# Final sum on 128 partitions with x1 and L stored channel by channel; v tiles asked for first while mixing

## What is computed

```python
x = x + L0(gn(x))      # gn: group norm, 16 groups of 3 channels, no affine
x = x + L1(gn(x))

# L0: qkv = 3x3 depthwise(1x1(x)); q, k, v in 8 heads of 6 channels, each 4x4 pixel
#     block unfolded to 96 rows per head x 16384 columns; q, k normalised along columns
attn = softmax(einsum('bhcn,bhdn->bhcd', q, k) * temperature)   # 96 x 96 per head
out  = einsum('bhcd,bhdn->bhcn', attn, v)                       # then fold back, 1x1 projection

# L1: four scans of 512 steps, each step a 5-tap convolution over the other axis
nxt = inp + conv1d(carry, w, b)    # down, then up (rows); right, then left (columns)
```

## Time and profile before

| | |
|---|---|
| median of 3 runs | 11776.97 us (11760.05 to 11849.2) |
| the profiled execution | 11759.42 us, span 11757.6 us |
| PE, DVE, ACT, POOL busy | 81%, 72%, 58%, 24% of the span |
| DMA, mean over the span | 187 GB/s (2199.76 MB) |
| mean granted TensorE clock | 0.913 |

### The profile page before, as it was taken

The page is one execution under the profiler, slowest core; times in us unless marked ns, Lnnn a source line. Parts: engine busy times, 40 slices in busy tenths (PEclk is TensorE's granted clock), DMA queues, the critical chain, the costliest instruction groups (busy, mean ns, idle before and its releaser), DMA issues. The chain is left out here.

```text
span 11757.6 us, 213657 instructions
## 1 busy us (share of the span) xinstructions
PE 9564.5 (81%) x72742; PEld 9137.6 (78%) x72742; DVE 8439.2 (72%) x15908; ACT 6855.6 (58%) x11561; POOL 2842.7 (24%) x4104
## 2 busy tenths in 40 slices
PE   0899999999999978878689989998999899980000
PEld 0899999999999966656489989998899899980000
DVE  8677777777777756656677777776899877765445
ACT  0677777677777733323266658998333366654444
POOL 0000000000000000000056656665566566650000
PEclk9999999999999988888899999999999999995555
DMA  8666666666666659988766657776666567769999
GB/s 346 120 131 132 132 129 132 120 132 130 133 130 131 132 124 207 213 189 204 176 200 208 217 184 194 209 212 175 200 207 218 181 196 211 212 196 290 281 272 278
DMA packets 697798, 2199.76 MB, mean 187 GB/s; under 512 B 57233, under 2 KB 549489, under 8 KB 602657
## 3 DMA queue, kind: packets, MB, share of 16 engines
q1 hardware_dynamic: 597344, 2097.84, 69.3%
q10 hardware_dynamic: 100352, 100.67, 3.4%
HBM read 1409.77 MB, written 788.53 MB: 187 GB/s over the span
## 5 line engine op out<-in xcount | busy, mean ns | idle before, releaser
L1193 POOL TENSOR_TENSOR down_lo<-down_o_t,down_hi 112x256 fp32r<-112x256 f32 x1024 | 706.4, 690 | 5978.7 <-ACT down_hi L1238 5586.9
L472 PE MATMUL conv_ps<-tap_high,x_high 128*128 128x432 f32 (+2 forms) x6144 | 1884.6, 307 | 43.9 <-DVE x_edge L548 30.1
L472 PE MATMUL conv_ps<-tap_low,x_high 128*128 128x432 f32 (+2 forms) x6144 | 1908.1, 311 | 0.0
L472 PE MATMUL conv_ps<-tap_high,x_low 128*128 128x432 f32 (+2 forms) x6144 | 1906.4, 310 | 0.0
L352 ACT ACTIVATE x_high<-raw,negmean 128x512 fp32r<-128x512 f32 x1024 | 1214.6, 1243 | 61.2 <-DMA raw_edge<-x 49.4
L544 DVE SCALAR_TENSOR_TENSOR x_low<-raw,negmean,x_high 128x512 fp32r<-128x512 f32 x1024 | 1148.6, 1150 | 120.8 <-ACT x_high L352 120.8
L472 PEld LDWEIGHTS conv_ps<-tap_high,x_high 128*128 128x128 f32 x6144 | 1161.6, 189 | 66.1 <-DVE x_edge L548 31.7
L472 PEld LDWEIGHTS conv_ps<-tap_high,x_low 128*128 128x128 f32 x6144 | 1166.4, 190 | 22.5
L472 PEld LDWEIGHTS conv_ps<-tap_low,x_high 128*128 128x128 f32 x6144 | 1162.8, 189 | 20.7 <-issue 0.2
L1363 DVE TENSOR_TENSOR fin_out<-fin_rows,fin_l 48x2048 f32<-48x2048 f32 x256 | 585.2, 2286 | 623.0 <-DMA out<-fin_out 352.5
L883 DVE TENSOR_TENSOR scan_t_b<-o_ps,res_b 48x1024 f32<-48x1024 f32 x512 | 625.7, 1222 | 560.7 <-PE o_ps L796 557.1
(11 more groups left out here) (191 smaller groups left out, 26410.6 us busy)
## 6 DMA issues: line engine op xcount, KB each, us to landing
raw<-x SPq DMA_DIRECT2D x764, 256.0 KB, 5.5
x_scan<-scan_t_b SPq DMA_DIRECT2D x64, 1792.0 KB, 16.5
down_u_in<-x_scan SPq DMA_DIRECT2D x64, 1792.0 KB, 15.4
d_rows<-down_o_t SPq DMA_DIRECT2D x32, 3584.0 KB, 24.3
u_cols<-up_o_t SPq DMA_DIRECT2D x64, 1792.0 KB, 14.5
right_u_in<-u_cols SPq DMA_DIRECT2D x32, 3584.0 KB, 16.6
r_cols<-right_o_t SPq DMA_DIRECT2D x32, 3584.0 KB, 24.4
left_u_in<-r_cols SPq DMA_DIRECT2D x32, 3584.0 KB, 16.7
```

Source lines behind the costliest of these rows:

```text
L472: nc.tensor.matmul(bank(dy, side, lo - side, hi - side), xs[at], ws[taps], start=fresh[side], stop=False, skip_group_check=True)
L1193: nc.gpsimd.tensor_tensor(lo[:, b, 1:LP + 1], state(k // T, k, b), hi[:, b, k % 2, 1:LP + 1], ALU.subtract).then_inc(lo_ready[b], 1)
```

## The change

- `x1_scan` becomes (B, C, G, 2, T, W2) and `l_rows` (B, C, G, 2, W/T, 8, T): channel by channel, without dead rows. A channel's data is 1 MiB from the next one's. So the store of x1 (mixing) and the load of it (down) are DMAs of 48 partitions for each half, and left's store runs 512 bytes at a time.
- `final_sum` cuts x1, L and the result into 24 equal chunks of 4 MiB, each 128 partitions x 32 KB, adds them with four adds of 128x2048 per chunk, straight from x1's and L's order; ScalarE's copies are gone. Stores are issued from ScalarE's queue.
- Mixing: SyncE asks for v one group further ahead and before it waits for sums; the residual is loaded as two blocks of 8 whole rows, so a channel's part is one run of 16 KB; the sums become four adds of 48x512.
- The down scan clears the dead rows of `u_in` on GpSimd and loads its first groups before the taps.
- Tiles needed only before the scans are released there, so the final sum's tiles fit.

```diff
     d_rows = dram("d_rows", (G, PP, T, B, W2))
     u_cols = dram("u_cols", (G, PP, B, H // 2, T))
     r_cols = dram("r_cols", (G, PP, T, B, H // 2))
-    l_rows = dram("l_rows", (G // 2, PP, B, W // T, T, T))
+    l_rows = dram("l_rows", (B, C, G, 2, W // T, NP, T))
 
     with ExitStack() as whole:
...
                 def load_res(g, s):
-                    rows = x[b].rearrange("c (m two) w -> two c m w", two=2)
-                    for r in range(2):
-                        sp.dma_start(res[ODD * r:ODD * r + C, s], rows[r, :, bass.ds(NP * g, NP)]).then_inc(res_landed[s], 16)
+                    for half in range(2):
+                        sp.dma_start(res[ODD * half:ODD * half + C, s],
+                                     x[b, :, bass.ds(T * g + NP * half, NP)]).then_inc(res_landed[s], 16)
 
                 def store(g, s):
 
                     sp.wait_ge(summed, N * g + N)
-                    sp.dma_start(x1_scan[bass.ds(g, 1), b].rearrange("g p t w -> (g p) t w"), scan_t[:, s]).then_inc(scan_out[s], 16)
+                    for q in range(2):
+                        sp.dma_start(x1_scan[b, :, bass.ds(g, 1), q].rearrange("c g t w -> c (g t) w"),
+                                     scan_t[ODD * q:ODD * q + C, s]).then_inc(scan_out[s], 16)
...
+                load_v(1, 1)
                 load_res(0, 0)
-                load_v(1, 1)
+
+                sp.wait_ge(att_done, NB)
+                load_v(2, 0)
                 load_res(1, 1)
-                with sp.Fori(1, G // 2) as i:
+                with sp.Fori(1, G // 2 - 1) as i:
                     for s in range(2):
 
-                        sp.wait_ge(att_done, NB * (2 * i + s - 1))
-                        load_v(2 * i + s, s)
-
-                        sp.wait_ge(summed, N * (2 * i + s - 1))
+                        sp.wait_ge(att_done, NB * (2 * i + s))
+                        load_v(2 * i + s + 1, 1 - s)
+
+                        store(2 * i + s - 2, s)
                         load_res(2 * i + s, s)
-                        store(2 * i + s - 2, s)
+                sp.wait_ge(att_done, NB * (G - 2))
+                load_v(G - 1, 1)
+                for s in range(2):
+                    store(G - 4 + s, s)
+                    load_res(G - 2 + s, s)
...
                 def sums(g, s, dy):
-                    r, q0 = dy % 2, dy // 2
                     bank = 2 * (dy % 2)
                     v.wait_ge(o_done, NM * g + 2 * dy + 2)
-                    for q in range(2):
-                        ins = nc.vector.tensor_tensor(
-                            scan_t[ODD * q:ODD * q + C, s, dy:T:N].rearrange("p i (j two) -> p i j two", two=2),
-                            o_ps[ODD * q:ODD * q + C, bank:bank + 2].rearrange("p two (i j) -> p i j two", j=TOK),
-                            res[ODD * r:ODD * r + C, s, q0:NP:2, q:W:2].rearrange("p i (j two) -> p i j two", two=2), ALU.add)
+                    for half in range(2):
+                        for q in range(2):
+                            at = dy + NP * half
+                            ins = nc.vector.tensor_tensor(
+                                scan_t[ODD * q:ODD * q + C, s, at:at + N + 1:N].rearrange("p i (j two) -> p i j two", two=2),
+                                o_ps[ODD * q:ODD * q + C, bank:bank + 2, 2 * TOK * half:2 * TOK * (half + 1)]
+                                .rearrange("p two (i j) -> p i j two", j=TOK),
+                                res[ODD * half:ODD * half + C, s, dy:NP:N, q:W:2].rearrange("p i (j two) -> p i j two", two=2),
...
-        LOADS = 2 if way in ("down", "up") else 1
-        STORES = 2 if way in ("up", "left") else 1
+        LOADS = {"down": 4, "up": 2}.get(way, 1)
+        STORES = {"up": 2, "left": 4}.get(way, 1)
...
                     if way == "down":
                         for b in range(B):
-                            sp.dma_start(u_in[:, s].rearrange("p (b x) -> p b x", b=B)[:, b],
-                                         one(src, g)[:, b].rearrange("g p t n -> (g p) (t n)")).then_inc(loaded[s], 16)
+                            for q in range(2):
+                                sp.dma_start(u_in[ODD * q:ODD * q + C, s].rearrange("p (b x) -> p b x", b=B)[:, b],
+                                             src[b, :, bass.ds(g, 1), q].rearrange("c g t n -> c (g t n)")).then_inc(loaded[s], 16)
...
                     elif way == "left":
                         for b in range(B):
-                            tile = o_t[:, s].rearrange("p (b g x) -> p b g x", b=B, g=G // 2)[:, b]
-                            sp.dma_start(dst[:, :, b, bass.ds(g * -1 + (G - 1), 1)].rearrange("g p c h t -> p g (c h t)"),
-                                         tile).then_inc(stored[s], 16)
+                            for r in range(2):
+                                tile = o_t[ODD * r:ODD * r + C, s].rearrange("p (b g x) -> p b g x", b=B, g=G)[:, b]
+                                sp.dma_start(dst[b, :, :, r, bass.ds(g * -1 + (G - 1), 1)].rearrange("c g w h t -> c g (w h t)"),
+                                             tile).then_inc(stored[s], 16)
...
-                load(0, 0, first=True)
-                load(1, 1)
+                sp.wait_ge(cleared, 1)
+                if norm:
+                    for s in range(2):
+                        sp.wait_ge(between_clear, s + 1)
+                        load(s, s)
+                for r in range(2):
+                    sp.dma_start(b_sb[ODD * r:ODD * r + C], bias).then_inc(params, 16)
+                    for shift in range(3):
+                        for q in range(2):
+                            k = 2 * (shift - 1) + r - q + K // 2
...
+                if norm:
+                    for s in range(2):
+                        nc.gpsimd.memset(u_in[32:64, s], 0.0).then_inc(between_clear, 1)
...
+        xt = sb("fin_x", [FP, 2, 2, T, W2])
+        lt = sb("fin_l", [FP, 2, 2, W // T, NP, T])
+        o_t = sb("fin_out", [FP, 2, T, W])
...
+        x_runs = x1_scan.rearrange("b c g q t w -> (b c g q t w)").rearrange("(j p f) -> j p f", p=FP, f=RUN)
+        l_runs = l_rows.rearrange("b c g r w h t -> (b c g r w h t)").rearrange("(j p f) -> j p f", p=FP, f=RUN)
+        o_runs = out.rearrange("b c h w -> (b c h w)").rearrange("(j p f) -> j p f", p=FP, f=RUN)
...
+                def load(j, s):
+                    sp.dma_start(xt[:, s].rearrange("p q t w -> p (q t w)"),
+                                 x_runs[bass.ds(j, 1)].rearrange("j p f -> (j p) f")).then_inc(x_in[s], 16)
+                    sp.dma_start(lt[:, s].rearrange("p r c h t -> p (r c h t)"),
+                                 l_runs[bass.ds(j, 1)].rearrange("j p f -> (j p) f")).then_inc(l_in[s], 16)
+
+                for s in range(2):
+                    load(s, s)
+                with sp.Fori(1, NCH // 2) as i:
+                    for s in range(2):
+
+                        sp.wait_ge(added, 2 * i + s - 1)
+                        load(2 * i + s, s)
...
+                def store(j, s):
+
+                    act.wait_ge(added, j + 1)
+                    act.dma_start(o_runs[bass.ds(j, 1)].rearrange("j p f -> (j p) f"),
+                                  o_t[:, s].rearrange("p t w -> p (t w)")).then_inc(stored[s], 16)
+
+                with act.Fori(0, NCH // 2) as i:
+                    for s in range(2):
+                        store(2 * i + s, s)
...
+                def add(j, s, first):
+
+                    v.wait_ge(x_in[s], 8 * (j - s) + 16)
+                    v.wait_ge(l_in[s], 8 * (j - s) + 16)
+                    if not first:
+                        v.wait_ge(stored[s], 8 * (j - s))
+                    for r in range(2):
+                        for q in range(2):
                             ins = nc.vector.tensor_tensor(
-                                o_t[ODD * half:ODD * half + C, s, r:RH:2].rearrange("p h (c t) -> p h c t", t=T),
-                                rows_t[part, s, h:h + RH // 2].rearrange("p h (c t) -> p h c t", t=T),
-                                lt[part, b, :, NP * s + h:NP * s + h + RH // 2].rearrange("p c h t -> p h c t"), ALU.add)
+                                o_t[:, s, r:T:2, q:W:2].rearrange("p h (c m) -> p h c m", m=NP),
+                                xt[:, s, q, r:T:2].rearrange("p h (c m) -> p h c m", m=NP),
+                                lt[:, s, r, :, :, q:T:2].rearrange("p c h m -> p h c m"), ALU.add)
```

158 lines of the change are left out of this document (47 added, 111 removed).

## The result

| | before | after |
|---|---|---|
| median | 11768.51 us (11756.46 to 11849.2) | 10963.9 us (10953.86 to 10969.64) |
| ratio after/before | | 0.9302, 95% interval 0.9259 to 0.9344 |
| profiled execution | 11759.42 us, span 11757.6 | 10969.64 us, span 10967.6 |

The forecast was 11130 us with a range of 10910 to 11400. The same kernel in a later comparison gave 10963.21 us (ratio 0.9295, interval 0.928 to 0.931).

What follows compares the result with a forecast made beforehand. The prediction took mixing and the final sum as DMA-bound, the scans as compute-bound. From 11759 us it took 440 for the final sum and 192 for mixing, added 5 for left's last store: 11130 us, range 10910 to 11400.

Steps and rivals of the forecast that it cites:

- even a perfect order would leave mixing at 21.7 us a group: Mixing: DMA engines busy 43.3 of 47.6 us per two groups, so order alone could not go below 21.7 us a group.
- the dry time alone: Mixing: asking for v earlier removes only the dry stretches, 4.3 us in two groups.
- the residual's long runs: Mixing: residual in runs of 16 KB instead of 2 KB takes 9.5 us a group instead of 11.2.
- the store's new form: Mixing: x1 store as two DMAs of 48 partitions, 1.573 MB instead of 1.835, taken at 5.0 us a group.
- The compute-bound rival: Mixing: faster residual and store cut DMA to 17.4 us, so compute decides; 384 us less, 10940 us; chance 0.17.
- Its beat of 17.8 us: Mixing: group time if DMA were no bound, instead of 17.4 us, with VectorE's sums cut into four adds.
- PE's wait for v gone and DVE waiting for the residual instead: Sign in mixing's new profile: PE no longer waits for v, DVE waits for the residual or stored tiles.
- Final sum: Last stage: 24 steps of 128 partitions at 31.1 us, loads at 402 GB/s, adds hidden; 760 us against 1200, 440 less.
- Left's tail: End of left scan: 5 us added for left's longer last store.
- Down and left: Scans: down's 48-partition loads and left's 512-byte-run stores stay hidden behind compute, costed at nothing.
- Start of down: Down scan's start: loads ahead of taps, GpSimd's clearing of dead rows beside VectorE's 13.71 us clear; zero cost.
- Slower than before: Rival: 1 MiB pitch of x1 and L slows all moved transfers, at 120 GB/s giving 11990 us; chance 0.03.

Runs made afterwards that it cites:

- order-only kernel: Kernel before with only SyncE's new mixing order (v one group further ahead, x1 store ahead of the residual's load): 11460.38 us, mixing 1262.4 us.
- padding: Changed kernel with 32 KB unused behind each x1 channel in DRAM, final sum loading x1 in four DMAs of 32 partitions: 11295.83 us.
- two-queue kernel: Changed kernel with down's first loads split, partitions 0 to 47 from SyncE's queue and 64 to 111 from ScalarE's: 10956.43 us.

## Why the prediction was right, and where its steps were off

**Mixing, the step that failed: "even a perfect order would leave mixing at 21.7 us a group".** The gain was 192 us by the forecast and 336.6 measured. The step took the busy time of the DMA engines (0.91 of 47.6 us) as work that has to be done whatever the order, and then split it by three clean windows (141, 427, 258 GB/s). But a clean window prices a transfer that has the engines to itself, and the busy time was not fixed. With the very same transfers the order-only kernel moves its 4.98 MB a group at 264 GB/s, 18.9 us. The residual's price of 11.2 us, from 141 GB/s, does not fit in there beside 4.3 and 6.1 us. So the terms were mis-sized one by one: the order was costed at the dry time alone (2.15 us a group down to 0.2, about 125 us in all) and gave 304; the residual's long runs were to give 109 us and gave nothing that can be seen; the store's new form was to cost 0.7 us a group (5.0 for 4.3) and gave some 40 us.

The compute-bound rival had a chance of 0.17 and a time of 10940, nearer to the result than the forecast, and it was half right on the mechanism too. A group of after takes 18.5 us, and more than half of the groups (13 of 22 in the window) run at PE's beat of 17.4. The rest are longer: VectorE waits for the residual (69.0 us over the stage), empties its PSUM bank late, and PE waits for the bank (41.4 us). So compute sets the floor, and the waits for DMA, at a share of 0.97, come with the last 1 us a group on top. The rival's reason, a residual lifted to 240 GB/s by its long runs, did not show. Its beat of 17.8 us rests on a misreading: the 4.35 us between VectorE's sums before were taken for VectorE's own, but its idle time in them ends on PE. The beat was PE's. VectorE's adds did grow as forecast (689 ns, 691 forecast), to 4.24 us with the statistics, and stayed under PE's 4.36, so the beat stayed at 17.4.

"PE's wait for v gone and DVE waiting for the residual instead" came as written. The range held the time only because it took in the compute-bound case; by the terms of the sum itself the result is luck.

**Final sum, right, gain 44 us under-sized.** The form of the statistics pass was the right row to take. Only its 402 GB/s for loads and the 410 for stores turned out to be 432 with both together (over 600 us; 302.0 MB in the stage's 715.9 us are 422 with both ends), 29.8 us a step against 31.1. That lies at the lower bound that was given (29.5). That the adds would hide is right, 2287 ns each, and so is the queue that never dries (share 1.00).

**Left's tail**, +5 forecast, +5.2 measured. **Down and left** were costed at nothing, and no new wait came in: down 1093.7 against 1095.2. The share in down rose to 0.87, near the 31.3 of 34.3 us worked out for it.

**Start of down, wrong: "zero".** It cost 23.0 us. The step counted GpSimd's clearing as hidden beside VectorE's, which was right (13.78 and 13.71 us, ending within 6 us of each other). It never asked what stands behind the loads in the queue. The taps do, and the loads had just been made of 48-partition DMAs. At the residual's 141 GB/s, a row at hand, 6.29 MB would have been 44.6 us; the wait was 45.0.

**Slower than before** and its 1 MiB pitch. Only mixing, down and left touch x1 and L at that pitch; the final sum reads them contiguously, so its 432 GB/s say nothing about it. In mixing the rate rose to 254 GB/s with the store at that pitch, and for down's loads padding changed nothing. The feared 120 GB/s were not seen.

**Left open.** That the DMA engines move 230 to 236 GB/s while busy in the old order and 247 to 265 in the new ones was measured, give or take the few per cent of the share. Why was only argued: with more kinds of transfer in the queue, loads to 48 partitions run beside stores and loads to 96, as the two halves ran beside each other in the two-queue kernel. No run here splits the rate inside mixing by transfer. Nor is it settled why 96 partitions lose so much of the rate in the final sum; a residual or x1 store from a second queue inside mixing was not tried.
